# Causal attention on one core: the eight PSUM banks split four, two, two among scores, outputs and side products, in place of three, two, three

## The reference

```python
q = concat(nq @ w_dq_nope, rope(nq @ w_dq_rope))          # 32 + 64 numbers per head
a1 = _attn(q, k1, v1, causal=True)                        # "latent" keys and values
a2 = _attn(q, ks, vs, causal=False)                       # 64 selected tokens
a3 = _attn(q, kw, vw, causal=True)                        # "window" keys and values
out = g[:, 0] * a1 + g[:, 1] * a2 + g[:, 2] * a3          # then @ w_proj
```

## Time and profile before

| | |
|---|---|
| median of three runs | 2679.42 us |
| time of the profiled execution | 2683.18 us |
| its span, first to last instruction | 2681.2 us |
| PE busy | 2243.5 us, 84% of the span |
| DVE busy | 1868.2 us, 70% |
| ACT busy | 1713.2 us, 64% |
| POOL busy | 1655.0 us, 62% |
| mean granted clock of TensorE | 0.928 |

### The profile page before, as it was taken

One profiled execution on the slowest core, in us unless ns is written; L12 is line 12 of the kernel. 1 busy time (PEld: TensorE's weight loads), 2 busy tenths in 40 slices (PEclk: granted clock), 3 DMA queues, 4 the chain that ended last, 5 costly groups with the idle time before them and its releaser, 6 DMA issues. The chain is left out here.

```text
span 2681.2 us, 37397 instructions
## 1 busy us (share of the span) xinstructions
PE 2243.5 (84%) x11394; PEld 1845.2 (69%) x11394; DVE 1868.2 (70%) x3832; ACT 1713.2 (64%) x3574; POOL 1655.0 (62%) x1432
## 2 busy tenths in 40 slices
PE   0177569999999999999999999999999995738885
PEld 0164437877778787777878787777878874638885
DVE  2556358787877878787877878787787772555553
ACT  3433217767777776777777777777878775216663
POOL 5155416767676776767676776766667665007884
PEclk9985569999999999999999999999999997759998
DMA  9857635335152534424252532223212112516766
GB/s 383 325 190 248 200 101 138 81 83 126 37 141 44 140 67 112 104 59 116 64 142 47 136 85 78 66 64 66 60 40 62 21 30 50 170 55 189 211 193 171
DMA packets 199861, 314.81 MB, mean 117 GB/s; under 512 B 95916, under 2 KB 130220, under 8 KB 186732
## 3 DMA queue, kind: packets, MB, share of 16 engines
q1 hardware_dynamic: 189947, 298.23, 39.0%
q0 software_dynamic: 9712, 14.18, 2.8%
HBM read 210.20 MB, written 101.75 MB: 116 GB/s over the span
## 5 line engine op out<-in xcount | busy, mean ns | idle before, releaser
L1396 POOL TENSOR_TENSOR p_lo<-prob,p_hi 128x512 fp32r<-128x512 f32 (+2 forms) x960 | 1119.3, 1176 | 550.8 <-ACT p_hi L1480 516.9
L1478 ACT ACTIVATE prob<-ps_s 128x512 f32<-128x512 f32 (+4 forms) x1344 | 728.8, 542 | 432.2 <-DVE ps_s L1714 352.4
L1480 ACT ACTIVATE p_hi<-ps_s 128x512 fp32r<-128x512 f32 (+3 forms) x1344 | 729.8, 543 | 1.6
L1612 DVE TENSOR_REDUCE max_part<-ps_x 128x1 f32<-128x512 f32 x744 | 506.2, 686 | 51.8 <-PE ps_x L1524 44.0
L1396 DVE TENSOR_TENSOR p_lo<-prob,p_hi 128x512 fp32r<-128x512 f32 (+1 forms) x320 | 261.2, 816 | 13.0 <-ACT p_hi L1480 11.6
L1610 DVE CUSTOM_DVE_ANT_0 ps_x<-ps_x,before 128x128 f32<-128x128 f32 x496 | 243.6, 493 | 25.4 <-PE ps_x L1524 17.1
L1577 PE MATMUL ps_o<-p_hi,v_win 128*128 128x512 f32 (+3 forms) x640 | 237.5, 371 | 5.6 <-DVE p_lo L1396 5.6
L1714 DVE TENSOR_TENSOR ps_s<-ps_s,mask_kq 128x128 f32<-128x128 f32 x512 | 152.7, 301 | 126.1 <-PE ps_s L1496 120.2
L1577 PE MATMUL ps_o<-p_hi,v_lat 128*128 128x512 f32 (+3 forms) x640 | 236.1, 369 | 0.1
L1579 PE MATMUL ps_o<-p_lo,v_win 128*128 128x512 f32 (+3 forms) x640 | 236.1, 369 | 0.0
L1579 PE MATMUL ps_o<-p_lo,v_lat 128*128 128x512 f32 (+3 forms) x640 | 234.4, 366 | 0.0
(11 more groups left out here) (433 smaller groups left out, 5782.6 us busy)
## 6 DMA issues: line engine op xcount, KB each, us to landing
raw<-in_experts_w_dram SPq DMA_DIRECT2D x23, 1536.0 KB, 7.6
wbuf<-in_tok_weight_dram SPq DMA_DIRECT2D x16, 2000.0 KB, 16.9
head_first<-kw_scratch SPq DMA_DIRECT2D x72, 256.0 KB, 5.0
kw_scratch<-st_hi SPq DMA_DIRECT2D x48, 256.0 KB, 2.8
kw_scratch<-st_lo SPq DMA_DIRECT2D x48, 256.0 KB, 3.2
q_scratch<-st_hi SPq DMA_DIRECT2D x48, 256.0 KB, 4.6
q_scratch<-st_lo SPq DMA_DIRECT2D x48, 256.0 KB, 5.1
head_first<-q_scratch SPq DMA_DIRECT2D x48, 256.0 KB, 7.3
```

The lines of the kernel that those rows point to most:

```text
L1396: ns.tensor_tensor(upper if low else p_lo[:, i % LSLOTS, c:CH], prob[low:P, i % NPROB, c:CH], upper.bitcast(F32), ALU.subtract).then_inc(s ...
L1478: nc.scalar.activation(prob[low:P, i % NPROB, c:CH], ps_s[i % 3][low:P, c:CH], ACT.Exp, scale=SCALE).then_inc(s["p_full"], 1)
L1480: nc.scalar.activation(p_hi[:, i % SLOTS, c:CH], ps_s[i % 3][:, c:CH], ACT.Exp, scale=SCALE).then_inc(s["p_up"], 1)
L1612: ins = nc.vector.tensor_reduce(mpart[:, q, c:c + 1], bank[:, 0:w], axis=AX.X, op=ALU.max)
```

## The change

The scores get a fourth bank, and the side products lose their third. The output banks stay at two, so that eight are used as before. `NX` becomes 2, a new constant `NS_BANKS` is 4, and each `i % 3` and `i - 3` of the scores goes by it:

```diff
-NX = 3
+NX = 2
+NS_BANKS = 4
...
-        ps_s = [ctx.enter_context(nc.psum_tensor(f"ps_s{i}", [P, CH], F32)) for i in range(3)]
+        ps_s = [ctx.enter_context(nc.psum_tensor(f"ps_s{i}", [P, CH], F32)) for i in range(NS_BANKS)]
...
-            wait_unit(pe, "p_up", h, i - 3)
+            wait_unit(pe, "p_up", h, i - NS_BANKS)
...
-            bank = ps_s[i % 3]
+            bank = ps_s[i % NS_BANKS]
```

More of the change, by code:

```diff
@@ L1477, in _ @@
                     lower_done(act, h, i - NPROB)
-                    nc.scalar.activation(prob[low:P, i % NPROB, c:CH], ps_s[i % 3][low:P, c:CH], ACT.Exp, scale=SCALE).then_inc(s["p_full"], 1)
+                    nc.scalar.activation(prob[low:P, i % NPROB, c:CH], ps_s[i % NS_BANKS][low:P, c:CH], ACT.Exp, scale=SCALE).then_inc(s["p_full"], 1)
                     wait_unit(act, "pv", h, i - SLOTS)
-                    nc.scalar.activation(p_hi[:, i % SLOTS, c:CH], ps_s[i % 3][:, c:CH], ACT.Exp, scale=SCALE).then_inc(s["p_up"], 1)
+                    nc.scalar.activation(p_hi[:, i % SLOTS, c:CH], ps_s[i % NS_BANKS][:, c:CH], ACT.Exp, scale=SCALE).then_inc(s["p_up"], 1)
                     for t in AT.get((h, i - 2), ()):
@@ L1712, in _ @@
                         c = width(i)[0]
-                        cut = ps_s[i % 3][:, c:c + P]
+                        cut = ps_s[i % NS_BANKS][:, c:c + P]
                         nc.vector.tensor_tensor(cut, cut, g.mask_kq[:], ALU.add).then_inc(s["cut"], 1)
```

## The result

The changed kernel took **2846.44 us** as the median of four runs (2842.6 to 2853.71) against 2680.81 us for the kernel before: 1.062 times as long, with a 95% interval of 1.060 to 1.065. The profiled execution took 2849.06 us, 165.9 us more than that of before. The prediction had said 2826, in a range from 2745 to 2915.

What follows compares the result with a forecast made beforehand. PE was taken to bound the attention: 2683.2 us profiled, less 8.7 for the fourth scores bank, plus 155 for the lost side product bank, gives 2829.5, or 2826 us as a median 3.8 lower; range 2745 to 2915 us.

Steps and rivals of the forecast that it cites:

- PE bounds the attention and its waits add up: In the attention, PE (TensorE) sets the pace, busy 84% of the span; any PE wait is added to the time.
- The wait moves one side product earlier: With two side product banks, a load waits for the reading two back, not three; 1.62 us lost at 1850 us.
- the place of the earlier trace: Side product stall near 1850 us in head 12: load 2.23 us late, less 0.61 us present idle, 1.62 us lost.
- The sum of 155 us: Loss from the side products' third bank: 12 heads at 10.3 us plus 4 heads at 7.7 us.
- eight places at head 12's price of 1.29 us: Heads 0 to 11: two more stall places than head 12's six, at 1.29 us each, 10.3 us a head.
- the step that I had called a choice: Head 12: DVE's waits for ACT come later by PE's delay, so six places add up to 7.74 us.
- Near 1841 us: One of head 12's six side product places: 1.56 us lost, with no PE wait there before.
- The clock: TensorE's granted clock falling with longer PE stalls; 54 us, left out of the 2826 us forecast, chance 0.25.
- Rival 2: At PE's longer stalls the clock falls, 3.4 us once in each of 16 heads: 54 us, 2880 us; chance 0.25.
- The time: Whole kernel: median of 2826 us, range 2745 to 2915 us.
- The fourth bank of scores, 8.7 us: At the scores' ring, a fourth bank gives back all 8.7 us that PE waits for ACT.
- What was to be seen: Signs in the new profile: PE's waits for DVE 180 to 260 us, over 120 places, longest over 2 us; longer heads.

Runs made afterwards that it cites:

- experiment 5: Experiment 1's kernel with 369 idle matmuls into its free bank, ahead of the side products where PE is held longest: 2781.0 us, 1.038 times the kernel before.
- experiment 1: The changed kernel with three banks of scores instead of four, two of side products, one bank unused: 2844.6 us, 1.061 times the kernel before.

## Why the prediction was right, and where it was not

**PE bounds the attention and its waits add up:** right. The two kernels differ by 165.9 us. PE's waits in the attention are 169 us against 84 (all of its rows there, `p_hi`, low parts and transposes among them), which is 85 us. The clock takes up to 60 us more. A matmul that follows a wait shows 0.50 us where it is 0.40 in a stream, so that the 88 more places at which it restarts may cost 0.1 us each; that is an estimate, 9 us. These make 154 of 166 us, and 12 are left without a row.

**The wait moves one side product earlier:** right, as the place of the earlier trace rows shows in the changed kernel. Forecast there was a load 2.23 us late; its weight load stood 1.91 us, and PE idles for 1.77 us in place of 0.61, a net loss of 1.16 us where I had 1.62.

**The sum of 155 us:** mis-sized, nearly all of it in heads 0 to 11. The side products' waits grew by 106 us, and all of PE's waits by 85 us, where I had 155 and, less the 8.7 us, 146. In the last four heads, whose places I had worked out one by one, I had 4 x 7.7 = 31 us, and PE's idle time grew by 25.9. In heads 1 to 11 I had 11 x 10.3 = 113 us, and it grew by 54.5.

The step that failed there is the one from head 12 to the others: eight places at head 12's price of 1.29 us, which is net of head 12's short waits. In heads 1 to 11 PE already idled for 6.4 us a head, not 2.8, and stalls that stood there fell away when the new ones came one side product earlier. The place of the earlier trace rows in head 4, before and after:

```profile
912.58 0.50 PE L1524 MATMUL ps_x<-k_hi,head_first 96*128 96x512 f32 x1 [1.04 <-DVE max_part L1612]
963.55 0.80 PE L1525 MATMUL ps_x<-k_hi,head_first 96*128 96x512 f32 x1 [1.78 <-DVE max_part L1613]
```

The new stall is as long as in head 12, but the net loss is 0.74 us and not 1.16.

A smaller miss, 0.8 us of head 12's 7.7, is the step that I had called a choice: that DVE's waits for ACT come later by PE's whole delay, so that the six places add up. Near 1841 us DVE waited 0.77 us for ACT's copy in the kernel before:

```profile
1841.20 0.68 DVE L1673 TENSOR_TENSOR raw_o<-ps_o,low_sum 32x512 f32<-32x512 f32 x1 [0.77 <-ACT low_sum L1460]
```

In the changed kernel the same output waits 0.28 us, and PE stalls for 0.80 us where I had 1.56:

```profile
1975.49 0.68 DVE L1674 TENSOR_TENSOR raw_o<-ps_o,low_sum 32x512 f32<-32x512 f32 x1 [0.28 <-ACT low_sum L1461]
...
1976.95 0.50 PE L1525 MATMUL ps_x<-k_hi,head_first 96*128 96x512 f32 x1 [0.80 <-DVE max_part L1613]
```

PE's delay had eaten part of ACT's lateness there. At the place of the earlier trace rows it had not (1.31 us both times).

**The clock:** wrongly left out. Rival 2 had a chance of 0.25 and 54 us; a fall of the clock came, with up to 60 us, and experiment 5 shows that it is paid in time. I had held against it that DVE's backlog would cover a slower PE. But it did not come as Rival 2 priced it, at 3.4 us once in each of 16 heads. At that place in head 12 it took 4 x (0.15 + 0.28) = 1.7 us, in head 14 nothing, and the last four heads together lost about 463 x 0.01 = 5 us. Most of it, about 1425 x 0.04 = 57 us, fell in heads 1 to 11, which stall more often; before the change these lost 3.4 us behind the stall at 564.19 us and 1.7 us behind the one at 1041.39 us (0.73 and 0.84 in two windows), so half as much behind the second stall as the price taken from the first. The Trainium skill ("TensorE: Matmul & The Clock Gate", section "A second HAM failure mode: psum-queue depth-cycling") tells of a kernel whose clock went up and down as its PE idled briefly between groups of matmuls. This trace agrees with it (0.85 and 0.72 above), though not at every stall (1.00 in head 14).

**The time:** right by luck. A term too large by 50 to 60 us and a term left out of up to 60 us stood against each other, and both lie in the same heads: heads 1 to 11 grew by 116.0 us where I had 113, but half of that is slower matmuls and not waits.

**The fourth bank of scores, 8.7 us:** the wait is gone as forecast, but the bank is not what removed it (experiment 1).

**What was to be seen:** waits for DVE of 180 to 260 us: 168, just under. Over 120 places: 223. Longest over 2 us: 2.5, but 1.8 at the place of the earlier trace rows, for which I had 2.2. Head 12 of about 116 us: 118.9. Head 10 of about 129 us: 129.7, by the luck just told. Last four heads under 1.00 if the clock falls: 0.99. DVE's busy time at 1868 us: 1910; why it grew is open.

## What to carry to other kernels

The waits at a ring of buffers don't tell what a smaller ring costs. Take each use, find when the reader frees the buffer that the writer will now need, and compare with the start of the writer's instruction; take off the stalls that already stand there, in each kind of head by itself; then add what the clock of TensorE does at the stalls that become the longest. And before trading banks, look at what the late reader itself waits for: here one instruction on DVE, moved one unit later, was worth 36 us with three banks and 133 us with two.

## What the hardware showed that was not expected

A stall of PE of about 1.8 us is in most cases followed by a lower granted clock in the next few microseconds (0.85 and 0.72 in head 12, but 1.00 in head 14), and a stall of 1.24 us was too (0.58 in head 7). 27 or fewer idle matmuls a head, put into the longest stalls, make experiment 1's kernel 64 us faster although PE does more work. Stalls of up to 1.04 us in the kernel before, as at 1743.83 us, left it at 1.00: the whole head from 1636 us on has that clock.
